# Eight tiles instead of four in a turn of the closing loop of a mixture of experts

## The chip, the cores and the metric

One core of a Trainium2 chip runs one program. The metric is the device time of a launch in microseconds (us). The engines are TensorE (PE, with its weight loads as PEld), VectorE (DVE), ScalarE (ACT), GpSimd (POOL) and SyncE (SP). Each has a program of its own, with its own loops and branches; they meet at semaphores.

## The reference, cut to what matters

```python
x = x + attention(layernorm(x), context)        # linear attention, 16 heads; x is [16, 128, 256]
x_flat = layernorm(x).reshape(-1, 256)          # 2048 tokens
probs = softmax(x_flat @ gate_w)                # 8 experts
topk_w, topk_idx = top_k(probs, 2)              # the two best, weights normed to 1
h = silu(xe @ w1[e]) * (xe @ w3[e])             # 256 -> 896, for each token's two experts
y = h @ w2[e]                                   # 896 -> 256
x = x + sum_k topk_w[k] * y[k]
```

How many tokens an expert gets is known only at run time.

## The kernel before

The attention runs over eight pairs of 128-token tiles, written out without loops. While it runs, each token is scattered into buckets in memory, one bucket for each expert. Then the mixture works on tiles of 128 bucket rows. A tile `t` has these steps, in the function `mix` of each engine:

- PE: `hidden(t, 0)` and `hidden(t, 1)` (24 products each, line 814), `x_transposes(t + 1)` (line 792), `output(t - 1)` (21 products, line 833), `g_transposes(t)` (7, line 852).
- ACT: the silu of the products, `evacuate_x(t + 1)`, `evacuate_y(t - 1)` (line 1054), `load(t + 2)` (a DMA, line 1041), `high_g(t)` (line 1078). Where a tile is the first of an expert, it also rounds parts of the next expert's weights (line 1066), inside an `If`.
- DVE: gates (line 1329), `split_x` (1324), `low_g` (1335).
- POOL: adds the rows of tile `t - 1` to the output with an indirect DMA (line 496); where a tile is an expert's first, the low parts of weights (line 486), inside an `If`.

So the output of a tile is computed one tile later than its hidden layer, and the last one stands behind all loops: on PE in line 900 (`output(n - 1, ...)`), on ACT and POOL in `last_tile`, which tries four places with an `If` each (line 222).

Each of the 2048 tokens goes to two experts, so there are 4096 rows, which fill `SURE` = 32 tiles. The last tile of an expert is mostly not full, which takes up to `E` = 8 more, and `AHEAD` = 4 tiles are computed early, among the attention's last steps, so that `MOST` is 44. Tiles 0 to 7 are written out. Tiles 8 to 31 run in a loop of three turns with eight tiles each (line 203), which has no conditions around its tiles. Tiles from 32 on run in the closing loop (line 206): each tile loads its entry of the table `tab_active` (line 208) and stands in an `If` (line 209) inside the `If` of the tile ahead of it, four deep. When a tile isn't used, the engine jumps to the end of the turn. Nothing ends the loop early: every turn tests its first tile. With these inputs 35 tiles are used (the page shows 35 output adds), so tiles 32, 33 and 34 run, the test of tile 35 fails, and the two other turns fail at tiles 36 and 40. Every engine walks through these loops by itself.

The tables (`tab_row`, `tab_expert`, `tab_active` and others) have `TILES` = `MOST` + 2 entries. DVE computes them on one partition, in the lines 1457 to 1499, between the steps of the early tiles.

The number of instructions between the head and the branch back, counted in each engine's code (what stands in an `If` is counted, taken or not):

| engine | loop of line 203, eight tiles | closing loop, four tiles | one more tile of the closing loop |
|---|---|---|---|
| PE | 1237 | 641 | 159 |
| ACT | 442 | 242 | 60 |
| POOL | 241 | 141 | 35 |
| DVE | 66 | 54 | 13 |

PE's whole code has 7036 instructions. On each engine the closing loop stands directly behind the loop of line 203.

Of the kernel before, what the change touches and what calls it, by code (L numbers as in the profile page):

```python
# [15 lines left out]
E, M = 8, 896  # L16
# [8 lines left out]
AHEAD = len(EARLY)  # L25
LIMITS = {5: (P, 2 * P), 6: (2 * P, 2 * P)}
SURE = 2 * T // P
MOST = SURE + E + AHEAD
TILES = MOST + 2
W13, W2 = KD * M, MB * D  # L30
WALL = 2 * W13 + W2
# [14 lines left out]
def build(nc, x, ctxT, maskT, wqT, bq, wkT, bk, wvT, bv, bdq, bdk, woT, bo, gate, w1, w2, w3, out):  # L46
    bucket = nc.dram_tensor("bucket", [PAD_AT + P, ROW], F32, kind="Internal").ap()

    with ExitStack() as stack:
# [35 lines left out]
        def lend(n):  # L85
# [57 lines left out]
        lists = kf[0:1, 1, 0:7 * TILES].rearrange("a (i t) -> a i t", i=7)  # L143
        active, is_last = lists[:, 5, :], lists[:, 6, 0:MOST]
        tab_row, tab_expert, tab_first, tab_active = (
            kf[0:1, 1, (7 + i) * TILES:(8 + i) * TILES].bitcast(I32) for i in range(4))
# [51 lines left out]
        def tiles_of_mixture(eng, step):  # L198


            for t in range(AHEAD + 1, 8):
                step(t, t % 4)
            with eng.Fori(1, SURE // 8) as r:
                for i in range(8):
                    step(8 * r + i, i % 4)
            with eng.Fori(SURE // 4, MOST // 4) as r:
                def tile_if_used(i):
                    go = eng.value_load(tab_active[0:1, bass.ds(4 * r + i, 1)], min_val=0, max_val=1)
                    with eng.If(go):
                        step(4 * r + i, i)  # L210
                        if i < 3:
                            tile_if_used(i + 1)

                tile_if_used(0)
# [13 lines left out]
        def tiles_used(eng):  # L228

            return eng.value_load(tab_used[0:1, 0:1], min_val=0, max_val=MOST - SURE) + SURE  # L230

# [144 lines left out]
        def _(pool):  # L376
# [159 lines left out]
            n, places = tiles_used(pool), last_places(pool)  # L536
            mix(AHEAD, 0)
            tiles_of_mixture(pool, mix)
            last_tile(pool, n, places, lambda n, v: add(n - 1, v))
            pool.wait_ge(y_added, 16 * n)  # L540

        @block.tensor
        def _(pe):
# [352 lines left out]
            pe.wait_ge(list_ready, 7)  # L896
            n = tiles_used(pe)
            tiles_of_mixture(pe, mix)

            output(n - 1, (E - 1) % 2 * WALL)  # L900

        @block.scalar
        def _(act):
# [218 lines left out]
            mix(AHEAD, 0)  # L1122
            n, places = count
            tiles_of_mixture(act, mix)

            def drain(n, v):
# [9 lines left out]
        def _(dve):  # L1136
# [312 lines left out]
            def link(ins):  # L1449
                done[0] += 1  # L1450
                ins.then_inc(list_step, 1)
                dve.wait_ge(list_step, done[0])
# [33 lines left out]
            link(nc.vector.tensor_scalar(used[:, 1:2], used[:, 0:1], -float(SURE), None, ALU.add))  # L1486
            link(nc.vector.tensor_tensor(is_last, active[:, 0:MOST], active[:, 1:MOST + 1], ALU.subtract))
            link(nc.vector.tensor_reduce(last_of[:], is_last.rearrange("a (j v) -> a v j", v=4), AX.X, ALU.add))
# [46 lines left out]
```

## Time and profile before

| what | us |
|---|---|
| median of three runs | 468.08 (465.04 to 470.28) |
| the profiled execution | 464.74 |
| its span, first to last instruction | 463.0 |
| PE busy | 428.7 (93%) |
| ACT busy | 230.9 (50%) |
| POOL busy | 213.3 (46%) |
| DVE busy | 209.6 (45%) |

The page counts matrix work and element work as busy, but no register, branch, semaphore or DMA-issuing instruction. A loop's own cost therefore shows as idle time of an engine, and in views that list sequencer instructions (their engines are written with a q: ACTq). "issue" in the chain of waits is time in which an engine waited for nothing that the profile shows. Reading a trace for this kernel means to find places where all engines stand still at once.

### The profile page before, as it was taken

The numbers are of one execution on the slowest core, as the hardware profiler recorded it, in microseconds if no ns is written. First come the engines' busy times: TensorE is split into PE (matmuls) and PEld (weight loads), VectorE is DVE, ScalarE is ACT, GpSimd is POOL, SyncE is SP. The second block draws the span as 40 slices with busy tenths as digits, with TensorE's granted clock in tenths as the row PEclk, the third lists the DMA queues.
The fourth block names the chain that finished last, engine by engine and source line by source line (L and its number), as shares of the span: only waits on it lengthen the run. The fifth ranks groups of instructions, "written<-read, shape, count | busy, mean of one in ns | idle before, by whom it ended". The sixth has DMA issues, their size and how long they took to land.

```text
span 463.0 us, 12218 instructions
## 1 busy us (share of the span) xinstructions
PE 428.7 (93%) x3921; PEld 396.0 (86%) x3922; DVE 209.6 (45%) x582; ACT 230.9 (50%) x477; POOL 213.3 (46%) x209
## 2 busy tenths in 40 slices
PE   3899999999999999989999998999999999999970
PEld 3789988898988888979999898899999899999970
DVE  4457788758876784323233331333232333233220
ACT  3677777578865523745333732553272373333320
POOL 4424375657434641798321671482177177121121
PEclk9999999999999999999999999899999999999996
DMA  8644121462128448335731236118121121121121
GB/s 255 195 134 156 47 70 48 145 234 70 49 59 286 114 128 260 80 122 168 256 54 24 37 110 187 23 35 272 23 43 29 23 39 30 23 46 23 36 37 11
DMA packets 34523, 46.10 MB, mean 100 GB/s; under 512 B 3488, under 2 KB 29344, under 8 KB 34464
## 3 DMA queue, kind: packets, MB, share of 16 engines
q1 hardware_dynamic: 22304, 31.82, 20.6%
q0 software_dynamic: 6576, 8.82, 11.3%
q10 hardware_dynamic: 5584, 4.76, 3.7%
q8 instruction: 27, 0.44, 0.4%
q14 instruction: 32, 0.26, 0.2%
HBM read 32.63 MB, written 12.76 MB: 98 GB/s over the span
## 4 chain that ended last, share of the span: by engine, by line
PE 68%; DVE 9%; issue 6%; POOL 5%; DMA 4%; ACT 2%; ACTq 1%; POOLq 1%; DVEq 0%
PE bank L814 28%; PE twin L833 15%; PE bank L852 4%; DMA out_rows<-qf,x_all 3%; POOL w_lo L486 3%; PE twin L667 3%; PE bank L547 3%; PE bank L548 2%; PE bank L549 2%; DVE w_lo L1229 2%; PE bank L593 2%; PE twin L679 2%; PE bank L571 2%; PE twin L792 1%; PE bank L610 1%
## 5 line engine op out<-in xcount | busy, mean ns | idle before, releaser
L496 POOL DMA_INDIRECT out_rows<-qf,x_all x35 | 54.6, 1559 | 147.4 <-ACT qf L1054 111.7
L814 PE MATMUL bank<-w_hi,c_hi 128*128 (+1 forms) x280 | 106.4, 380 | 3.8 <-issue 2.0
L814 PE MATMUL bank<-w_lo,c_hi 128*128 (+1 forms) x280 | 103.0, 368 | 0.0
L833 PE MATMUL twin<-w_hi,kv_halves 128*128 (+1 forms) x490 | 95.2, 286 | 2.9 <-DVE kv_halves L1335 2.4
L1329 DVE TENSOR_TENSOR x_all<-bank,x_all 128x448 f32<-128x448 f32 x70 | 43.4, 623 | 97.3 <-ACT x_all L1073 97.2
L486 POOL TENSOR_TENSOR w_lo<-raw,w_hi x18 | 76.0, 4422 | 12.8 <-ACT w_hi L1066 10.1
L1335 DVE TENSOR_TENSOR kv_halves<-bank,kv_halves 128x512 fp32r<-128x512 f32 x66 | 38.6, 623 | 93.9 <-ACT kv_halves L1078 93.9
L833 PEld LDWEIGHTS twin<-w_hi,kv_halves 128*128 128x128 f32 x490 | 77.5, 188 | 3.7 <-DVE kv_halves L1335 2.6
L814 PE MATMUL bank<-w_hi,c_lo 128*128 (+1 forms) x280 | 79.9, 367 | 0.0
L1073 ACT ACTIVATE x_all<-bank 128x448 f32<-128x448 f32 x70 | 37.8, 544 | 80.6 <-PE bank L814 70.1
L833 PE MATMUL twin<-w_lo,kv_halves 128*128 (+1 forms) x245 | 68.7, 280 | 0.0
L814 PEld LDWEIGHTS bank<-w_hi,c_hi 128*128 128x128 f32 x280 | 53.1, 190 | 9.6 <-issue 5.6
L814 PEld LDWEIGHTS bank<-w_hi,c_lo 128*128 128x128 f32 x280 | 52.9, 189 | 4.5
L814 PEld LDWEIGHTS bank<-w_lo,c_hi 128*128 128x128 f32 x280 | 53.3, 190 | 3.6
L1078 ACT CAST kv_halves<-bank 128x512 fp32r<-128x512 f32 x66 | 32.4, 540 | 29.6 <-PE bank L852 22.8
L1054 ACT ACTIVATE qf<-twin,x_all 128x256 f32<-128x256 f32 x35 | 16.6, 476 | 60.2 <-PE twin L833 60.2
L833 PEld LDWEIGHTS twin<-w_lo,kv_halves 128*128 128x128 f32 x245 | 46.3, 189 | 0.1
L428 POOL DMA_INDIRECT bucket<-rows,slot x32 | 36.8, 1150 | 16.2 <-DVE slot L1320 8.5
L852 PE MATMUL bank<-ident,x_all 128*128 128x128 f32 x233 | 32.4, 274 | 3.7 <-DVE x_all L1329 3.7
L1066 ACT CAST w_hi<-raw x36 | 32.0, 939 | 6.1 <-issue 4.3
L852 PEld LDWEIGHTS bank<-ident,x_all 128*128 128x128 f32 x233 | 26.2, 140 | 5.3 <-DVE x_all L1329 5.2
L379 POOL TENSOR_SCALAR rs<-mv 128x2 f32<-128x2 f32 (+2 forms) x12 | 2.8, 231 | 50.0 <-DVE mv L1193 33.7
(219 smaller groups left out, 703.4 us busy)
## 6 DMA issues: line engine op xcount, KB each, us to landing
raw<-in_w SPq DMA_DIRECT2D x24, 896.0 KB
x_all<-bucket ACTq DMA_DIRECT2D x31, 129.0 KB, 2.1
raw<-in_ctxT SPq DMA_DIRECT2D x8, 256.0 KB, 2.9
out_rows<-x_all SPq DMA_DIRECT2D x8, 256.0 KB, 2.1
bucket<-pad_rows SPq DMA_DIRECT2D x13, 129.0 KB, 2.4
x_all<-in_x SPq DMA_DIRECT2D x2, 512.0 KB, 6.4
x_all<-bucket SPq DMA_DIRECT2D x6, 129.0 KB, 2.7
x_all<-in_x SPq DMA_DIRECT2D x1, 768.0 KB, 6.3
```

Source lines behind the costliest of these rows:

```text
L428: pool.indirect_dma_start(out=bucket, out_offset=bass.IndirectOffsetOnAxis(ap=slot[:, o, k:k + 1], axis=0), in_=rows[i % 2][:, o, k, :], i ...
L486: return pool.tensor_tensor(w_lo[:, bass.ds(at + i * W13, W13)], raw[:, bass.ds(at + i * W13, W13)], w_hi[:, bass.ds(at + i * W13, W13)].b ...
L496: pool.indirect_dma_start(out=out, out_offset=bass.IndirectOffsetOnAxis(ap=x_in[:, v, D:D + 1].bitcast(U32), axis=0), in_=y[:, v, :], in_o ...
L814: last = nc.tensor.matmul(bank[b][:, 0:MC], stationary[:, k, :], w[:, bass.ds(at + (of + k * M + c * MC), MC)], start=(k == 0 and part == ...
L833: last = nc.tensor.matmul(bank[6][:, 0:D], stationary[:, k, :], w[:, bass.ds(at + (2 * W13 + k * D), D)], start=(k == 0 and part == 0 and ...
L852: last = nc.tensor.transpose(b[:, at:at + P], g[:, k * P:(k + 1) * P], ident[:])
L1054: nc.scalar.activation(y[:, v, :], bank[6][:, 0:D], ACT.Copy, scale=x_in[:, v, D + 1:ROW]).then_inc(y_ready, 1)
L1066: nc.scalar.copy(w_hi[:, bass.ds(at + of, PIECE)], raw[:, bass.ds(at + of, PIECE)]).then_inc(hi_ready, 1)
L1073: nc.scalar.activation(silu[:, c, :], bank[c][:, 0:MC], ACT.Silu).then_inc(silu_ready, 1)
L1078: nc.scalar.copy(g_hi[:, k:end, :].rearrange("p k n -> p (k n)"), b[:, 0:(end - k) * P]).then_inc(g_hi_ready, 1)
L1329: nc.vector.tensor_tensor(g[:, c * MC:(c + 1) * MC], bank[2 + c][:, 0:MC], silu[:, c, :], ALU.mult).then_inc(g_ready, 1)
L1335: nc.vector.tensor_tensor(g_lo[:, k:end, :].rearrange("p k n -> p (k n)"), b[:, 0:(end - k) * P], g_hi[:, k:end, :].rearrange("p k n -> p ...
```

## The change

`MOST` grows from 44 to 48 tiles, and with it `TILES` from 46 to 50. The closing loop has two turns of eight tiles, nested eight deep, and not three turns of four. The loop of line 203 stays, and so does all that stands ahead of it.

```diff
-MOST = SURE + E + AHEAD
+MOST = SURE + 2 * E
 TILES = MOST + 2
...
-            with eng.Fori(SURE // 4, MOST // 4) as r:
+            with eng.Fori(SURE // 8, MOST // 8) as r:
                 def tile_if_used(i):
-                    go = eng.value_load(tab_active[0:1, bass.ds(4 * r + i, 1)], min_val=0, max_val=1)
+                    go = eng.value_load(tab_active[0:1, bass.ds(8 * r + i, 1)], min_val=0, max_val=1)
                     with eng.If(go):
-                        step(4 * r + i, i)
-                        if i < 3:
+                        step(8 * r + i, i % 4)
+                        if i < 7:
                             tile_if_used(i + 1)
```

## Rows read from the trace of the kernel before

**Rows 1.** The page: span, busy time, the chain that ended last by engine.
```profile
span 463.0 us, 12218 instructions
PE 428.7 (93%) x3921; PEld 396.0 (86%) x3922; DVE 209.6 (45%) x582; ACT 230.9 (50%) x477; POOL 213.3 (46%) x209
PE 68%; DVE 9%; issue 6%; POOL 5%; DMA 4%; ACT 2%; ACTq 1%; POOLq 1%; DVEq 0%
```

**Rows 2.** Chain of waits, line 203's second turn begins (start us, us, what).
```profile
282.38 0.04 ACTq L203
...
283.09 1.95 issue
285.05 0.07 ACTq L203
285.11 2.46 issue
287.58 0.29 ACTq L1083
...
290.85 0.47 issue
291.32 6.69 PE bank L814 x24
...
301.46 4.87 PE bank L814 x24
```

**Rows 3.** Chain of waits, the third turn begins.
```profile
353.13 0.04 ACTq L203
...
355.61 0.07 ACTq L203
355.68 2.34 issue
358.02 0.29 ACTq L1083
```

**Rows 4.** Line 203 around the second turn, by engine (ns min/median/max, first and last start).
```profile
L203 PEldq COMPARE_BRANCH  x1: 261/261/261, 278.3 to 278.3; - x1
L203 PEldq FUSED_REGOPS  x1: 68/68/68, 278.6 to 278.6; - x1
...
L203 POOLq COMPARE_BRANCH  x1: 45/45/45, 282.4 to 282.4; - x1
...
L203 POOLq FUSED_REGOPS  x1: 68/68/68, 282.7 to 282.7; - x1
```

**Rows 5.** DMA queues that carry instructions, the whole span (packets, MB, share of 16 engines).
```profile
q8 instruction: 27, 0.44, 0.4%
q14 instruction: 32, 0.26, 0.2%
```

**Rows 6.** DMA queues from 282 to 290.5 us.
```profile
q14 instruction: 3, 0.02, 0.8%
```

**Rows 7.** Lines 206 (444 to 453 us) and 222, the walk out of the closing loop.
```profile
L206 PEldq ALU_OP  x3: 36/36/36, 445.5 to 448.5; - x3
L206 PEldq COMPARE_BRANCH  x3: 76/214/224, 445.6 to 448.6; - x3
...
L206 POOLq ALU_OP  x3: 32/32/35, 448.0 to 450.4; - x3
...
L206 ACTq ALU_OP  x3: 35/35/38, 448.4 to 450.8; - x3
L206 ACTq COMPARE_BRANCH  x3: 40/45/45, 448.5 to 450.9; - x3
...
L206 ACTq FUSED_REGOPS  x2: 68/68/68, 448.7 to 449.9; - x2
...
L222 ACTq COMPARE_BRANCH  x4: 40/45/45, 451.0 to 452.0; - x4
```

**Rows 8.** Chain of waits, the last tile.
```profile
447.76 0.45 DVE kv_halves L1335
448.21 0.03 issue
448.25 0.30 DVEq L208
448.55 0.38 DVE kv_halves L1335
448.93 2.75 PE twin L833 x21
451.68 0.02 issue
451.70 0.04 ACTq L1053
451.74 0.05 issue
451.79 0.48 ACT qf L1054
...
453.17 1.55 POOL out_rows L496
```

**Rows 9.** Busy time by stretch (us, PE, PEld, DVE, ACT, POOL, granted clock, DMA, GB/s).
```profile
291.40:294.80 3.40, 3.40 (x10) 3.02 (x11) 0.93 (x2) 1.90 (x3) 1.11 (x2) 0.50 0.37 39
295.00:298.00 3.00, 3.00 (x18) 2.73 (x16) 0.62 (x1) 1.94 (x3) 3.00 (x1) 1.00 0.00 0
448.90:451.70 2.80, 2.75 (x21) 2.55 (x21) 0.02 (x1) 0.00 (x0) 0.00 (x0) 1.00 0.46 50
455.30:463.00 7.70, 0.00 (x0) 0.00 (x0) 0.00 (x0) 0.00 (x0) 0.00 (x0) 0.50 0.15 17
```

**Rows 10.** DVE in order of time, two of the table's steps.
```profile
163.63 0.27 DVE L1458 TENSOR_TENSOR qf<-n_row,steps 1x128 f32<-1x128 f32 x1
168.71 0.52 DVE L1470 TENSOR_TENSOR qf<-tile_no,ends 1x368 f32<-1x368 f32 x1
```

## What the change will do to the time

> **What bounds the kernel now.** I began with the page. PE is busy for 93% of the span, and the chain that ended last runs on PE for 68% of it [rows 1]. For most of the run the time is the number of products, and the change leaves all of them. So I asked where PE stands still, and read the chain of waits around the places where the loops turn. The reader is to see two things there.
>
> The first is at the turns of line 203. ACT takes the branch back at 282.4 us, its next instruction starts at 285.05, and after that single instruction it stands again until 287.58; nothing that the profile shows holds it [rows 2]. One turn later the same: 353.15 to 355.61, then 355.68 to 358.02 [rows 3]. These are about 2.6, 2.5, 2.4 and 2.3 us. PE and POOL take the same branch back within 0.3 us [rows 4]. The queues that carry instructions explain it: q14 moved 32 packets with 0.26 MB, so 8 KB each, q8 27 packets with 0.44 MB, so 16 KB each [rows 5]. PE's code has 7036 instructions; over 27 packets that is 260 for each, so q8 is PE's, a block of it holds about 256 instructions, and a block of q14 (the other engines') about 128. Between 282 and 290.5 us q14 moved three packets [rows 6]. I read: an engine keeps a few blocks around the place where it is and has the next one fetched when it enters a block. ACT's turn of 442 instructions is 3.5 blocks, the head is gone when it jumps back, and it waits for the head's block. The second wait, one instruction later, says that the head is the last instruction of its block. PE's turn of 1237 instructions is 4.8 of its larger blocks and is still there.
>
> The second is the end. PE computes the last output from 448.93 on [rows 8]. Ahead of it, it walks out of the closing loop: its three turns end between 445.5 and 448.5, which is 1.5 us for a turn, 1.2 us on ACT and POOL [rows 7]. ACT's branches back there cost 0.2 to 0.3 us (448.5 to 448.7) [rows 7]: 242 instructions are under two blocks. PE, ACT and POOL all come out of the loop just before they are needed.
>
> **The change, part by part.** All that stands ahead of the closing loop keeps its length, so the tiles up to 31 and both stalls of line 203 stay. Tiles 32 to 34 do the same work in the same nest, and fall through from one to the next. Cost: nothing.
>
> *One turn less.* After tile 34 the test of tile 35 fails, and then one more turn fails (at tile 40) where two did. PE saves 1.5 us, ACT and POOL 1.2 us [rows 7].
>
> *Longer jumps.* A tile more is 159 instructions on PE and 60 on ACT. The turn is then 1277 on PE and 482 on ACT. There are three jumps now: from tile 35's test to the end of the turn, back to the head, and from tile 40's test to the end again.
>
> ACT: count from the block border that [rows 2] place behind the head of line 203. The closing loop begins 442 instructions later, in the fourth block. Tile 35's test is near 627, in the fifth block (512 to 639). The turn ended near 684, in the sixth, which is fetched when the fifth is entered. It now ends near 924, in the eighth. That block was never asked for, so the jump waits for it. The jump back is 482 instructions, longer than the 442 that stalled. The jump to the end again is a third one, if the wait drops what was kept: the three packets [rows 6] cover the head's block, the next, and one after that which would still have been near, so I take it that it does. A stall adds 2.0 to 2.4 us to a normal branch [rows 2, 3, 7]; I take 2.3. ACT: 3 x 2.3 - 1.2 = +5.7 us.
>
> PE: from tile 35's test to the end there are 5 x 159 = 795 instructions, 3.1 blocks; only the next block is fetched ahead. So this jump stalls. The jump back is 1277 instructions, and a turn of 1237 fits, but if a jump outside drops what was kept, as on ACT, the head is gone, and at tile 40's test the end is too. That is three stalls. What one costs on PE the trace does not show. Below, it is nothing (if the block is there after all); the nearest rows are ACT's 2.3 us. A block of PE is larger: 0.4% of 16 engines' 463 us over 27 packets is 1.1 us each, against 0.2% over 32, 0.46 us, for the others [rows 1, 5], which makes 2.3 + 0.6 = 2.9, say 3.0 us. Above, I allow 4.0, if a fetch waits for one more block of 1.1 us that the jump made useless. I take 3.0, as it is worked out from both. PE: 3 x 3.0 - 1.5 = +7.5 us, so the last output starts at about 456.4.
>
> POOL: 5 x 35 = 175 instructions forward, 279 back: at most one stall, and its walk out ended at 450.4 [rows 7], while the add starts at 453.17 [rows 8]. That covers it, above all when PE is late. DVE: a turn of 106 instructions is under one block. Nothing.
>
> *The clock.* PE now stands still from 446.6 to 456.4. The granted clock was 0.50, so the lower level of 1.2 GHz, from 291.4 to 294.8, after the pauses around 289 us, and again from 455.3 on, after PE's last work at 451.7 [rows 9]. The 24 products that began at the lower clock took 6.69 us against 4.87 [rows 2], so 1.8 us more. The last output (2.75 us at full clock [rows 8, 9]) begins after nearly 10 us without work, so I add 1.8 us; nothing if the clock holds.
>
> *What hides what.* The last copy of ACT (line 1054) needs PE's output and ACT out of its loop. PE's output: 451.68 + 7.5 + 1.8 = 461.0. ACT comes past the loop and three of the four branches of line 222 at about 451.4 [rows 7]: + 5.7 = 457.1. PE comes last, ACT's stalls lie beside PE's. If PE's weren't there, ACT's would show: 457.1 against 451.7 is +5.4.
>
> *The tables.* Four DVE steps go from 368 to 400 elements. From 128 to 368 elements a step grew by 0.25 us [rows 10], about 1 ns for each, so 4 x 0.03 = 0.13 us, and some 15 steps over 46 entries grow by 4 ns each. Below 0.2 us together, and before 175 us it lies ahead of a pause of DVE. I take 0.
>
> **Sum:** +7.5 + 1.8 = +9.3 us. The profiled execution had 464.74 us around its span of 463.0, so 474.0 for a like one. The median of the runs shown is 3.3 us above it, 468.08; on that scale 477.4 us.
>
> The Trainium skill (Runtime: NRT & Kernel Launch, section Instruction fetch mechanics) says that a taken branch whose target is outside the current two-page window forces a fetch before execution goes on. The direction agrees with [rows 2]; the window doesn't, since PE's branch back over 4.8 blocks took 0.3 us [rows 4], and by two pages it would have stalled. By that rule alone the jumps counted above would all stall as well, and the sum would be the same.
>
> **Rivals.**
>
> *ACT sets the end (chance 0.22).* PE keeps its old blocks when it jumps ahead, so it has one stall: 3.0 - 1.5 = +1.5, out at 450.4. Then ACT is last: +5.4, so 473.5 us. For it: PE holds at least five blocks. Against it: ACT fetched blocks again that it had had.
>
> *Stalls that queue up (0.07).* Each useless fetch of the next block delays the one that is wanted: 3 x 4.0 - 1.5 + 1.8 = +12.3, 480.4 us.
>
> *No stall to speak of (0.16).* The fetch runs far enough ahead for the jumps of both engines, or the target is fetched while the engines still work at 445 to 448.5 us. Then the turn saved is what is left: PE would wait for DVE's first half (448.2 to 448.5 [rows 8]) and start up to 0.5 us earlier, 467.6 us. That is not slower. It decides if the first jump on PE costs less than 1.5 us. Against it: ACT's stalls hid behind nothing.
>
> *The forecast (0.55):* three stalls on PE, 474.5 to 479.5 us.
>
> **How the numbers follow.** The likeliest case gives 477.4. From 471.5 to 481 the range takes in the ACT case and the queued one; left out is most of the case without stalls. About 1% (4.7 us) is what a measurement can tell from no change here. Slower by more: the forecast and the queued case nearly whole, and two thirds of the ACT case, 0.76. The rest is within 1%, 0.20, but for 0.04 kept for faster by over 1%, for which I found no mechanism.
>
> **What would show it.** At the end of the trace after: line 206 with two passes on each engine and not three; behind the branches of line 209 and 206 gaps of 2.3 us on ACT and about 3 us on PE; more packets on q8 and q14 than 27 and 32 (each refetch is one); the output's 21 products at a granted clock of 0.50; and all times up to about 445 us as before. The prediction is wrong if these gaps are missing, if only the first one is there on PE, or if the extra time lies before 445 us.

## The result and the profile after

| what | before | changed kernel |
|---|---|---|
| median, 22 runs each | 467.97 us | 471.8 us |
| ratio after / before | | 1.009 (95%: 1.0061 to 1.0118) |
| span of the profiled execution | 463.0 us | 470.1 us |

The change costs 0.9%, about 4.2 us. The ratio and its interval leave out the few runs of either kernel that were in the slower state of the chip; the medians are of all 22. The two profiled executions differ by 7.1 us, so more is in them than the change. I cut both into three stretches: up to PE's entry into the loop of line 203, from there to ACT's first copy of the last tile (line 1078), and the tail behind it. In the rows of busy time (columns as in [rows 9]) the kernel before has

```profile
0.00:210.40 210.40, 194.15 (x2426) 176.01 (x2428) 134.77 (x445) 132.17 (x285) 111.53 (x166) 1.00 0.44 138
210.40:447.10 236.70, 231.80 (x1476) 217.41 (x1474) 73.67 (x136) 97.25 (x189) 98.64 (x41) 0.99 0.30 70
447.10:463.00 15.90, 2.75 (x21) 2.55 (x21) 1.16 (x2) 1.44 (x3) 3.10 (x2) 0.76 0.19 25
```

and the changed kernel

```profile
0.00:214.60 214.60, 197.16 (x2426) 178.77 (x2428) 134.81 (x445) 131.85 (x285) 111.70 (x166) 0.98 0.43 135
214.60:450.10 235.50, 230.35 (x1476) 216.03 (x1474) 73.84 (x136) 97.08 (x189) 98.71 (x41) 1.00 0.30 71
450.10:470.10 20.00, 4.84 (x21) 4.55 (x21) 1.16 (x2) 1.44 (x3) 3.10 (x2) 0.63 0.15 23
```

The reader is to see the same number of instructions in each stretch and where the time differs. The first stretch is 4.2 us longer, in code that the change doesn't touch; the granted clock was 0.98 there. Over the executions of all kernels of this study it took from 210 to 219 us. That is scatter of the attention's part, and medians of many runs even it out. The middle is 1.2 us shorter: the kernel before had 3.4 us at the lower clock in it [rows 9]. The tail is 4.1 us longer, about the 4.2 us of the runs. The tail is what the change did. That the two numbers agree to 0.1 us is in part luck: the clock during the last output differs from one execution to the next by more than a microsecond (last section), and there is one profiled execution of each kernel here.

In the tail, the branches of lines 209 and 206 on the changed kernel (ns min/median/max, first and last start), which answer to [rows 7]:

```profile
L209 PEldq COMPARE_BRANCH  x2: 213/1865/3517, 448.2 to 453.2; - x2
L209 POOLq COMPARE_BRANCH  x2: 45/45/45, 450.9 to 452.3; - x2
L209 ACTq COMPARE_BRANCH  x2: 45/45/45, 451.0 to 457.6; - x2
...
L206 PEldq ALU_OP  x2: 36/36/36, 451.8 to 453.5; - x2
L206 PEldq COMPARE_BRANCH  x2: 76/160/244, 451.9 to 453.6; - x2
...
L206 ACTq ALU_OP  x2: 35/36/38, 453.9 to 457.8; - x2
L206 ACTq COMPARE_BRANCH  x2: 40/42/45, 454.0 to 457.9; - x2
...
L206 PEldq FUSED_REGOPS  x1: 68/68/68, 452.2 to 452.2; - x1
...
L206 ACTq FUSED_REGOPS  x1: 68/68/68, 456.9 to 456.9; - x1
```

PE's branch out of tile 35's test takes 3.52 us (448.2 to 451.8). Its branch back takes 0.3 us (451.9 to 452.2), and the second jump out (453.2) 0.3 us again. ACT jumps at 451.0 and goes on at 453.9, jumps back at 454.0 and goes on at 456.9, and its last jump out (457.6 to 457.8) is a normal one. So there is one stall on PE and there are two on ACT. The chain of waits of the changed kernel:

```profile
450.79 0.45 DVE kv_halves L1335
451.24 0.04 issue
451.28 0.31 DVEq L208
451.58 0.37 DVE kv_halves L1335
451.96 2.00 issue
453.95 4.86 PE twin L833 x21
458.81 0.02 issue
458.83 0.04 ACTq L1053
458.87 0.05 issue
458.92 0.48 ACT qf L1054
```

Beside [rows 8]: 2.00 us of issue where there was none, and 21 products in 4.86 us and not 2.75. Their clock:

```profile
451.85:458.67 6.82, 4.72 (x21) 4.55 (x21) 0.10 (x1) 0.00 (x0) 0.01 (x1) 0.50 0.20 28
```

The clock stood at its lower level, 1.2 GHz (0.50), through nearly all of the output. The two terms are 2.0 + 2.1 = 4.1 us, all that the tail grew by. The instruction queues moved one packet more on q8 and four more on q14 than in [rows 5]:

```profile
q8 instruction: 28, 0.46, 0.4%
q14 instruction: 36, 0.29, 0.2%
```

### The profile page after: what moved, and what is told of

The parts are those of the page before. It is cut to its first block, busy times and chain, and to the rows that moved or that the text cites. A ratio compares the mean times of both kernels' runs of the same rounds, so it can differ in the third digit from the quotient of the medians.

```text
span 470.1 us, 12190 instructions
## 1 busy us (share of the span) xinstructions
PE 432.4 (92%) x3921; PEld 399.4 (85%) x3922; DVE 209.8 (45%) x582; ACT 230.4 (49%) x477; POOL 213.5 (45%) x209
## 4 chain that ended last, share of the span: by engine, by line
PE 70%; DVE 9%; issue 6%; POOL 5%; DMA 3%; ACT 3%; ACTq 1%; POOLq 1%; DVEq 0%
PE bank L814 28%; PE twin L833 15%; PE bank L852 4%; POOL w_lo L486 3%; PE twin L667 3%; PE bank L547 3%; DMA out_rows<-qf,x_all 2%; PE bank L549 2%; PE bank L548 2%; DVE w_lo L1229 2%; PE bank L593 2%; PE twin L679 2%; PE bank L571 2%; PE bank L610 2%; PE twin L792 1%
## 5 line engine op out<-in xcount | busy, mean ns | idle before, releaser
L833 PE MATMUL twin<-w_hi,kv_halves 128*128 (+1 forms) x490 | 97.2, 290 | 5.3 <-issue 5.2
L833 PEld LDWEIGHTS twin<-w_hi,kv_halves 128*128 128x128 f32 x490 | 79.2, 192 | 6.3 <-issue 6.2
```

The lines of the kernel that those rows point to most:

```text
L833: last = nc.tensor.matmul(bank[6][:, 0:D], stationary[:, k, :], w[:, bass.ds(at + (2 * W13 + k * D), D)], start=(k == 0 and part == 0 and ...
```

## The experiments

All stretches below are cut as above. "Tail" is from ACT's first copy of the last tile to the end of the span: 15.8 us before, 19.9 us in the changed kernel.

### Which engine's loop costs the time

In the first, `MOST` is 48 and each engine's closing loop takes its own size; PE alone goes back to three turns of four.

```diff
-            tiles_of_mixture(pe, mix)
+            tiles_of_mixture(pe, mix, turn=4, end=MOST - 4)
```

> The changed kernel, but PE's closing loop has three turns of four tiles again; ACT, POOL and DVE keep two turns of eight. Theory (each engine waits for blocks of code at its own long jumps, and either engine alone is late enough): PE's walk out loses its gap of 3.5 us, its last output starts about 0.1 us after DVE's halves, as before, at full clock (2.75 us and not 4.9), but ACT still waits 2.9 us twice, so the copy of line 1054 comes at ACT's own time, 8.2 us after the first copy of line 1078 of that tile, against 4.65 us before and 8.75 us in the changed kernel: +3.6 us against the kernel before. Rival (PE's wait and its clock alone make the time): 4.65 us, time as before.

Measured: ratio 1.0048 (1.0009 to 1.0087). PE's gap is gone, its output starts at 448.56, 0.50 us behind the end of DVE's first half. ACT's two stalls stay, and its copy comes 7.85 us after its first one (8.2 expected; the first stall was 2.4 and not 2.9 us). The rival is refuted: without PE's stall the tail is still 3.1 us longer than before (18.9 us). One part of the expectation failed: the output took 4.17 us, not 2.75. Its clock fell although PE had stood no longer than before:

```profile
448.50:452.75 4.25, 4.17 (x21) 3.98 (x21) 0.03 (x1) 0.00 (x0) 0.00 (x0) 0.61 0.30 37
```

The same for ACT alone:

```diff
-            tiles_of_mixture(act, mix)
+            tiles_of_mixture(act, mix, turn=4, end=MOST - 4)
```

> The changed kernel, but ACT's closing loop has three turns of four tiles again; PE, POOL and DVE keep two turns of eight. Theory: ACT's two gaps of 2.9 us go, PE's gap of 3.5 us and its lower clock stay, and the copy of line 1054 comes 8.7 us after the first copy of line 1078: +4.1 us against the kernel before. Rival (ACT's waits alone make the time): 4.65 us, time as before.

Measured: ratio 1.007 (1.0046 to 1.0095), tail 19.4 us. Chain of waits of this kernel (line numbers are two lower than in the changed one):

```profile
449.73 1.48 issue
451.20 4.86 PE twin L831 x21
```

PE's stall (a branch of 3.34 us) and the lower clock carry nearly the whole loss by themselves: 8.2 us from ACT's first copy to its last, 8.7 expected. Together with the run before: either engine alone is late enough, and their losses lie beside each other.

Both back to four:

> The changed kernel with three turns of four tiles on PE and on ACT; POOL and DVE keep two turns of eight, and the tables have 50 entries. Theory: 4.65 us from the first copy of line 1078 to line 1054, and the time of the kernel before within 0.5 us. Rival (the longer tables, or the loops of POOL and DVE, carry part of the time): 1 us or more above the kernel before.

Measured: ratio 0.9989 (0.9969 to 1.0009), tail 15.75 us, 4.65 us from the first copy to line 1054, exactly as before. Longer tables, and the loops of POOL and DVE, cost nothing that can be measured. q14 moved 33 packets here, against 32 before and 36 in the changed kernel, so three of its four further packets were ACT's.

### Is it the length of the jump or the number of jumps?

```diff
-            with eng.Fori(SURE // 4, MOST // 4) as r:
+            turn = MOST - SURE
+            with eng.Fori(1, 2) as r:
...
-                        step(4 * r + i, i)
-                        if i < 3:
+                        step(turn * r + (SURE - turn + i), i % 4)
+                        if i < turn - 1:
```

> The kernel before with the closing loop as one turn of twelve tiles, nested twelve deep, on all engines. The jump out from tile 35 is the longest yet (9 tiles), but it is the only one. Theory (a price for each jump into a block that isn't there, whatever its length): one gap of 3.5 us on PE and of 2.9 us on ACT and two turns fewer, which gives PE +3.2 - 3.0 = +0.2 us and ACT +2.5 - 2.4 = +0.1 us; the time of the kernel before within 0.6 us, with the output at full clock. Rival (what costs is the length of the jump or of the turn): at least the 4 us of the changed kernel.

Measured: ratio 0.9995 (0.9967 to 1.0023). The nest of twelve is longer in code than that of eight and costs nothing that can be measured. The one jump took 3.76 us on PE and 2.7 us on ACT. The profiled execution had a tail of 17.9 us all the same: the output started 0.66 us later behind DVE than before, and its clock fell (4.12 us). So this kernel's tail is 2.1 us longer in that one execution, while its ten runs show no loss; what they leave room for is about 1 us. Neither the depth of the nest nor a still longer jump makes the loss of the changed kernel. What that kernel has and this one doesn't is a second turn behind the jump that misses: 1.8 us on PE, a second stall on ACT.

### What the kernel keeps of its code, tried on the loop of line 203

The kernel before showed pairs of stalls on ACT at each turn of that loop [rows 2, 3]. Three edits of ACT alone, each on the kernel before. First, six turns of four tiles:

```diff
-            with eng.Fori(1, SURE // 8) as r:
-                for i in range(8):
-                    step(8 * r + i, i % 4)
+            with eng.Fori(8 // sure, SURE // sure) as r:     # sure is 4 on ACT, 8 elsewhere
+                for i in range(sure):
+                    step(sure * r + i, i % 4)
```

> The kernel before, but on ACT the loop of the tiles 8 to 31 has six turns of four tiles (222 instructions between head and branch) and not three of eight (442). PE, POOL, DVE and the closing loop as before. Theory (ACT keeps its last four blocks of 128 instructions; a turn that spans no more finds its head): no gap of 2.3 to 2.6 us on ACT at any turn, where the kernel before has two pairs. The first pair cost PE 1.9 us idle, 0.3 us of issue and 1.8 us at the lower clock, the second pair about 1 us: 5 us less, 463 us on the scale of the 468 us. Rival (ACT's gaps at the turns are hidden or come from something else, such as the weights' transfer): time as before.

Measured: ratio 0.9878 (0.9831 to 0.9925). On ACT all five branches back go on within 0.3 us. The middle stretch takes 231.9 us and not 236.7. q14 moved 18 packets and not 32.

Second, the turn of eight with a prefetch hint:

```diff
-            with eng.Fori(1, SURE // 8) as r:
+            with nc.Fori(1, SURE // 8, engines=[mybir.EngineType.Activation], hint_back_edge=True) as r:   # on ACT
```

> The kernel before, but ACT's loop of the tiles 8 to 31 carries a prefetch hint for its branch back: one instruction at the top of each turn that names the branch. The turn stays at eight tiles. Theory (the gaps are fetches of code): the gap behind the branch goes from 2.6 us to the 0.3 us of other branches, the one behind the first instruction may stay (2.3 us) since only the head's block is named; 3 to 5 us less than before. Rival (the gaps are no fetches): both gaps stay, time as before.

Measured: ratio 0.9923 (0.9889 to 0.9957). Line 206 is the loop here, at the second turn:

```profile
L206 ACTq COMPARE_BRANCH  x1: 78/78/78, 284.8 to 284.8; - x1
...
L206 ACTq BRANCH_PREFETCH_HINT  x1: 41/41/41, 285.0 to 285.0; - x1
L206 ACTq FUSED_REGOPS  x1: 68/68/68, 285.1 to 285.1; - x1
```

Both gaps are gone, the second too, of which I had expected that it may stay. One instruction that names the branch ahead of time takes 5 us of stall away, so the gaps are fetches of code. The packets tell more: from 278 to 414 us, a stretch with both branches back of the loop, q14 moved 11 packets in the kernel before and none in this one (20 in the whole span, not 32). So the hint didn't fetch the head's block early. The blocks of the turn were still there, and nothing was fetched again. Middle stretch: 232.0 us.

Third, the head shifted by four instructions:

```diff
+            for _ in range(8):
+                act.wait_ge(list_ready, 7)
             tiles_of_mixture(act, mix)
```

The trace shows these eight waits as four instructions, at 187.6 to 187.9 us.

> The kernel before with four more instructions on ACT (waits that are already met) ahead of the loop of the tiles 8 to 31. Theory (the loop's first instruction is the last of its block, so each turn waits for two blocks one after the other): the head moves into the next block, the gap behind the branch stays at 2.4 to 2.6 us, the gap behind the first instruction goes, and the time falls by 2 to 4 us. Rival (both gaps belong to the branch back whatever its place): both stay.

Measured: ratio 0.9904 (0.9864 to 0.9945).

```profile
L203 ACTq COMPARE_BRANCH  x1: 45/45/45, 285.8 to 285.8; - x1
...
L203 ACTq FUSED_REGOPS  x1: 68/68/68, 288.4 to 288.4; - x1
```

```profile
L1083 ACTq TENSOR_LOAD <-kf x1: 293/293/293, 288.5 to 288.5; - x1
```

The stall behind the branch stays (2.6 us), the one behind the first instruction is gone (288.4 to 288.5). The reading of [rows 2], that the head was the last instruction of its block, holds, and the four instructions gain about 1%, as much as the other two edits within their intervals. Middle stretch: 233.1 us.

### How much PE keeps

PE's loop of line 203 with two turns of twelve tiles, the rest as before:

> The kernel before, but PE's loop of the tiles 8 to 31 has two turns of twelve tiles (1852 instructions, 7.2 blocks of 256) and not three of eight (1237, 4.8 blocks). Theory (PE keeps its last eight blocks, one of them the next): the one branch back, near tile 20 at about 315 us, finds its head gone and shows a gap of 3.3 to 3.6 us; the time rises by 2 to 4 us. Rival (PE keeps more, or the price in the changed kernel came from jumping forward only): the branch back takes 0.3 us, time as before.

Measured: ratio 1.0125 (1.005 to 1.02).

```profile
L203 PEldq COMPARE_BRANCH  x1: 6317/6317/6317, 321.5 to 321.5; - x1
L203 PEldq FUSED_REGOPS  x1: 68/68/68, 327.9 to 327.9; - x1
```

A turn of 7.2 blocks doesn't find its head, where 4.8 and 5.0 blocks did. The stall is 6.3 us and not the 3.3 to 3.6 expected. q8 moved 38 packets. The rows of busy time around this stall, and around PE's jump in the changed kernel below it:

```profile
322.00:330.00 8.00, 2.50 (x17) 2.18 (x16) 1.15 (x2) 1.44 (x3) 1.55 (x1) 0.84 0.90 279
448.85:451.95 3.10, 0.73 (x7) 0.49 (x5) 1.16 (x2) 1.44 (x3) 1.55 (x1) 0.98 0.19 51
```

The last two columns are the DMA engines' busy share and GB/s. The branch of 6.3 us fell into a transfer of the weights on q1, and the first packet of q8 started only at 325.5 us, 4.0 us behind the branch; in the changed kernel it started at 449.2, 1.0 us behind the jump, and so it did in the kernels of twelve tiles and of ACT at four. The 3.0 us between them are about the 2.8 us by which this stall is longer. So what it has beyond the others was most likely the wait of its fetch among other transfers; this is one branch in one execution.

### The hint in the changed kernel

```diff
-            with eng.Fori(SURE // 8, MOST // 8) as r:
+            with nc.Fori(SURE // 8, MOST // 8, engines=[mybir.EngineType.Activation], hint_back_edge=True) as r:   # on ACT
```

> The changed kernel with a prefetch hint for the branch back of ACT's closing loop alone. Theory (two gaps on ACT, one forward, one back, each a fetch): the gap behind the test of tile 35 stays at 2.4 to 2.9 us, the one behind the branch back falls to about 0.3 us if the named block is still there after the jump, and stays if the jump dropped it. Time as the changed kernel, since PE's one gap and its lower clock carry the end by themselves. Rival: both gaps stay or both go.

Measured, in one execution that is compared with no run of the kernel before: the jump out took 2.6 us, the branch back 0.23 us, so the second of ACT's two stalls goes and the first stays. 470.7 us, tail 18.5 us; PE's jump still takes 3.3 us, and most of the 1.4 us against the changed kernel's tail is the clock, which fell during the output (3.63 us) and not ahead of it.

### A version that beats both

ACT's loop in six turns of four, and the closing loop left after the last used tile:

```diff
-            with eng.Fori(SURE // turn, end // turn) as r:
+            last = MOST // turn if n is None else eng.snap((n + 3) // 4)     # n: tiles used, on PE, ACT, POOL
+            with eng.Fori(SURE // turn, last) as r:
```

> The kernel before with ACT's loop of the tiles 8 to 31 in six turns of four tiles, and with PE, ACT and POOL leaving the closing loop (three turns of four at most) after the turn that holds the last used tile, by the number of tiles that they have loaded anyway. Theory: no gaps on ACT at the turns, 3 to 5.7 us as in the run of six turns of four; at the end PE is out of its loop at its first pass of the loop's end and not its third, 3 us earlier, so that the last output starts when DVE's first half is there, up to 0.4 us earlier than before. Together 1.0 to 1.3% below the kernel before. Rival (the walk out of the loop already sets the end by more than that): a further 1 us.

Measured: 0.9954 (0.9921 to 0.9987), a smaller gain than the 0.9878 of the loop of four alone. The profiled execution reached the loop only at 219 us and had 17 us at the lower clock in the attention's part, so both were run once more, side by side.

> The kernel before with ACT's loop of the tiles 8 to 31 in six turns of four, once more, beside the next kernel on the same chip. Theory: the stretch from PE's entry into that loop to ACT's first copy of the last tile's line 1078 takes 232 to 233 us, against 236 to 237 us in the kernel before; ratio 0.985 to 0.993. Rival (the gain of the first run was scatter of the attention's part, where the clock falls at times): ratio 0.995 or above, the stretch as before.

> The same with the early way out of the closing loop, once more. Theory: the stretch again 232 to 233 us, the last output within 0.1 us behind DVE's first half, so the ratio is that of the kernel beside it or 0.001 lower. Rival (loading the number of turns into the loops costs something before the end): the ratio is again 0.004 or more above it.

Measured: 0.9936 (0.99 to 0.9972) and 0.9942 (0.9907 to 0.9977).

```profile
215.80:447.95 232.15, 229.15 (x1476) 215.99 (x1474) 73.99 (x136) 97.23 (x189) 98.81 (x43) 1.00 0.31 71
447.95:463.40 15.45, 2.75 (x21) 2.55 (x21) 1.16 (x2) 1.44 (x3) 2.96 (x2) 0.74 0.18 26
```

This is the loop of four alone: 232.15 us for the middle in this execution too, against 236.70 before, with PE busy for 229.15 and not 231.80. The early way out adds nothing to be measured: the output started 0.05 us behind DVE's first half, against 0.47 in the kernel before and 0.18 in the one beside it, but the ratios are equal. So the difference of the first pair of ratios is best taken for scatter. What can be said is a gain of 0.5 to 1.2%, from ACT's loop alone.

## Why the prediction was wrong

Its direction and mechanism held, its size did not: +9.3 us forecast, +4.2 us measured. 471.8 us is inside the range, at its very edge, only because the range reached down for the case in which ACT sets the end; the forecast itself was 474.5 to 479.5 us.

- **Where the time goes.** Right. All of it lies behind the last tile's work, in the walk out of the closing loop. The stretches ahead have it in neither direction, and with PE and ACT back at four the time is that of the kernel before.
- **Price of a stall.** Near. PE's jump took 3.52 us against 0.36 us before, +3.2 us (3.0 said, worked out from ACT's gaps and the larger block). ACT's were +2.5 and +2.7 us (2.3 said).
- **Number of stalls.** Wrong, and this is the step that failed. The prediction let a jump outside drop all that was kept, because ACT fetched three packets behind its branch back [rows 6], one for a block that "would still have been near". The trace shows one stall on PE and two on ACT; only the first one being there on PE is a sign that the prediction had named for being wrong. Its reading of the three packets was one of two. The other fits these counts: the engine keeps the blocks it fetched last, each new one pushing out the oldest, and has the next one fetched when it enters one. With four blocks on ACT, the block that was near at 282 us was pushed out by the two fetched ahead of it, and was fetched again. In the changed kernel the jump out and the block fetched behind it push out the head (second stall), while the end of the turn stays (no third one). PE's turn of 5.0 blocks stays whole: one stall and not three. That takes 2 x 3.0 = 6.0 us out of the sum: 3.0 - 1.5 + 1.8 = +3.3, and with the measured sizes 2.0 + 2.1 = +4.1 us. The number of stalls is shown. The reason isn't: that it is four blocks, and a queue by age, is argued from these counts, and the run with the hint on line 203 doesn't fit it. There the hint stands where the head had stood, so by the reading of [rows 2] the turn lies in five blocks, and still none was fetched again. How many blocks ACT keeps, and which one it gives up, stays open.
- **The clock.** Near in these two executions, +1.8 said, +2.1 measured. But PE's pause was 4.4 us and not the 10 us that the prediction had counted: in the changed kernel and in the one with ACT at four (3.8 us) the output ran at 0.50 from its start (4.84 us). It isn't so every time: with the hint in the changed kernel, after 3.8 us too, the first product ran at full clock and the output took 3.63 us.
- **The turn saved.** 1.5 us said, 1.2 us came of it on PE: two turns of 1.5 us before, one of 1.8 us now, as its load of the table entry took 0.50 us and not 0.3. With the stall that is 3.2 - 1.2 = 2.0 us.
- **The rival "ACT sets the end".** It had the right count of PE's stalls, and the wrong clock: it left out that the clock can fall after one stall too. Without that PE would have been done at 456.7 and ACT would have set the end; with it PE was done at 458.81, and ACT stood ready at about 458.4. The two were 0.4 us apart, which is why putting one of them right regained 0.5 and 1.0 us of tail.
- **POOL, DVE, the tables:** nothing, as said.

The rule of the Trainium skill that the prediction weighed (Runtime: NRT & Kernel Launch, section Instruction fetch mechanics) gave the direction. Its window of two pages does not hold here: PE's branch back over 5.0 blocks took 0.3 us in the changed kernel, and over 7.2 blocks it stalled for 6.3 us.

## What to carry to other kernels

A loop has a size in code on each engine, and what counts is whether the branch back and the jump out land on blocks that are still or already there; a branch of 0.3 us became one of 2.4 to 3.8 us where they didn't, 6.3 us while the DMA engines were full, and no busy time shows it. Count the instructions of a turn on each engine, the untaken `If` bodies with them, and give each engine the turn that it can keep (or a hint): here the middle stretch took 234.8 to 237.3 us in the seven profiled executions with ACT's loop of line 203 as it was (and PE's too), and 231.9 to 233.1 us in the six with it mended, what it did to PE's clock included. Where two engines walk out of a loop side by side, mend both, since the losses hide each other.

## What the runs showed of the hardware that I had not expected

- One hint instruction per turn on ACT (0.04 us) removed two stalls of 2.3 to 2.6 us at each turn, and in the changed kernel the stall of the branch back (2.9 to 0.23 us). In the loop of line 203 it did so without any further fetch: q14, the instruction queue that ACT shares, moved nothing from 278 to 414 us.
- Four instructions ahead of a loop changed the time by 1% (0.9904), because the loop's head had been the last instruction of its block.
- PE's clock at the end is not fixed by its pause: after pauses of 2.2 to 2.4 us the output took 2.73 to 2.76 us in the kernel before and five others, and 3.8 to 4.3 us in four more. Two kernels were profiled twice, the one with ACT at four in line 203 and the one with the early way out, and each stands on both sides (4.13 and 2.75 us, 3.78 and 2.76 us).
- A stall of 6.3 us on PE's branch back over 7.2 blocks, against 3.3 to 3.8 us for every jump forward that missed: its fetch started 4.0 us behind the branch, while other transfers kept the DMA engines busy, and not 1.0 us.
